# Third attention of a four-stage kernel: rounded scores of four row blocks interleaved, maxima in bf16, one subtraction instruction

## The chip, the cores and the metric

The kernel runs on one core of a Trainium2 chip. The metric is the time of one execution on the device in microseconds (us). One execution was also recorded by the hardware profiler; its rows are what this document reads. Engines are named as in the profile: PE is the matrix engine (PEld its weight loads), DVE the vector engine, ACT the scalar engine, POOL the GpSimd engine, SP the engine that issues most DMAs.

## The reference, cut to what matters

The model is a chain of small blocks: two convolution-like attentions, an attention with a top-2 mixture of experts, and then the layer that the change is in, an attention over 512 tokens with 8 heads of width 16, again followed by a mixture of experts. Here the batch is seen as 8 images of 256 tokens. The kernel does for each of the 8 images (b), each of the 8 heads (h):

```
scores  = (q / sqrt(16)) @ k.T            # 256 x 256, float32 in the matrix engine
scores  = round_to_bf16(scores)
p       = exp(scores - max(scores, row))  # bf16
p       = p / sum(p, row)                 # sum kept as bf16
out     = p @ v                           # then the output projection, added to t
```

On the chip's side one row of scores is 256 numbers that lie on one partition, and 128 rows are handled at once. A head of an image is two such row blocks; the kernel takes two heads together, so a unit of work is four row blocks of 128 x 256 numbers.

## The kernel before, in words

**Tiling.** The third attention is `block4`. Its unit is a step (b, g): image b of 8, group g of 4, where a group is two heads, that is four row blocks r = 0..3. There are 32 steps. `images()` writes the first image out, loops images 1 to 5 with a hardware loop of four steps, and writes the last two images out. Two buffers (index g % 2) hold scores `s3`, probabilities `p3` and transposed probabilities `pT3`.

**What each engine does in a step, in its program order:**

- PE: `scores` of three steps ahead (L1698, L1699), `values` of the step before (L1726), in some steps the output transposes and projection (L1735, L1741, L1745), `transposed` of this step (L1710), `project` of q or k for a later fragment (L1684 to L1686).
- ACT: `rounded` of two steps ahead, one ACTIVATE of 1024 numbers per partition that copies the scores out of the PSUM banks as bf16 into `s3` (L1616); in three steps of four `evacuate`, which copies the transposed probabilities out (L1632); `upper` (L1608); `exponentials` of the next step, four ACTIVATEs of 256 numbers, each with a row sum into `smb3` (L1625).
- DVE: `centre` of the next step (L1816 takes the maximum of the two halves of each row into `mxh3`, L1818 reduces that to four maxima in `mx3`, L1821 subtracts them from `s3`, one instruction for each row block); in one step of four `evacuate` (L1836); `normalise` of this step (reciprocal L1826, four multiplications L1829); `lower` (L1808 or L1810); and one of `gather` (L1844), `copy_out` (L1852), `add` (L1857).
- POOL: `split_values`, once for an image (L1585 to L1591).

**What orders them.** The engines run their own lists and wait on semaphores: `sb` (a rounded score group is there), `sub` (a subtraction is done), `ex` (an exponential is done), `p` (a normalised row block), `tp` and `pt` (transposed, copied out). `exponentials` waits for all four subtractions (`sub` at 4i + 4) before its first ACTIVATE; `transposed` waits for all four multiplications. In `centre` DVE waits for itself twice, for the halves' maxima and for the four maxima.

**Layout.** `s3` is `[P, 2, 2 * S, N]`, so for a buffer each partition holds row block 0's 256 bf16 numbers, then row block 1's, and so on. `mxh3` is `[P, 4, 128]` in bf16, `mx3` is `[P, 4, 4]` in float32.

Of the kernel before, what the change touches and what calls it, by code (L numbers as in the profile page):

```python
# [16 lines left out]
BF16 = mybir.dt.bfloat16  # L17
U32, I32 = mybir.dt.uint32, mybir.dt.int32
ALU = mybir.AluOpType
ACT = mybir.ActivationFunctionType  # L20
AX = mybir.AxisListType

P = 128
B = 8
N = 256
S = N // P
T = B * N
H, DH = 8, 16
# [68 lines left out]
def build(nc, a, out):  # L97
    ctx = ExitStack()
    with ctx:
# [3 lines left out]
        def sem(name):  # L103
            return ctx.enter_context(nc.semaphore(name))

        ps = ctx.enter_context(nc.psum_tensor("ps", [P, 8, CH], F32))

        def psb(bank):

            return ps[:, bank, :].bitcast(BF16)  # L110
# [47 lines left out]
        def own(name, shape, dt=F32):  # L158
            return room.enter_context(nc.sbuf_tensor(name, shape, dt))
# [37 lines left out]
        chv, chp = Chain(None, dve_s), Chain(None, pool_s)  # L197
# [40 lines left out]
        @block.sync  # L238
        def _(sp):
            early = AT["bias1"][1]  # L240
            sp.dma_start(w[:, 0:early], a["pack"][:, 0:early]).then_inc(s_w, 16)
            for p in range(L):
                sp.dma_start(xs[:, p, :].rearrange("c (b n) -> c b n", b=2),
                             a["x"][2 * p:2 * p + 2].rearrange("b c n -> c b n")).then_inc(m[f"xs{p}"], 16)
            sp.dma_start(w[:, early:], a["pack"][:, early:]).then_inc(s_w2, 16)
            sp.dma_start(braw, a["b12"]).then_inc(s_braw, 16)

            sp.wait_ge(s_still, 1)
            sp.dma_start(xs_d[0:1], still[0:1, 0:P]).then_inc(s_braw, 16)
            sp.wait_ge(s_braw, 32)  # L250
# [316 lines left out]
        def flat(banks):  # L567
            return banks.rearrange("p a b -> p (a b)")
# [351 lines left out]
        def pair_high(act, c, cs=c3):  # L920

            act.wait_ge(cs["tp"], c + 1)
            act.activation(xH[:, c * CH:(c + 1) * CH], pair_bank(c, cs), ACT.Copy).then_inc(cs["xh"], 1)
# [25 lines left out]
        def weighted_rows(act, layer, c):  # L949

            act.wait_ge(gathered[c], (layer + 1) * 16 * 2)
            for b in (2 * c, 2 * c + 1):
                for s in range(S):
                    x = act.activation(y_rows(1, s, b), y_rows(1, s, b), ACT.Copy, scale=gk[:, row(layer, s, b), 1:2])
            x.then_inc(y_weighted, 1)
# [20 lines left out]
        def place(layer, r):  # L976
# [5 lines left out]
                     act=NT, hm=0, ht=NT, hH=NT, hL=NT, yp=NT, yo=NT, fin=0, ftp=0, fo=0, fst=0, oh=0)  # L982
# [6 lines left out]
        def experts(layer, wHL, n_up, hid, gate_w, gate_b):  # L989
# [326 lines left out]
            def _(dve):  # L1316
# [196 lines left out]
        v3f = own("v3f", [P, B, S, P])  # L1513
        v3r = own("v3r", [P, 2, S, P])
        vp3 = own("vp3", [P, B, S, H, 3, DH], BF16)
        mx3 = own("mx3", [P, H // 2, 2 * S])
        sm3 = own("sm3", [P, H // 2, 2 * S])
        smb3 = own("smb3", [P, H // 2, 2 * S], BF16)
        mxh3 = own("mxh3", [P, 2 * S, P], BF16)
        s3 = own("s3", [P, 2, 2 * S, N], BF16)  # L1520
        p3 = own("p3", [P, 2, 2 * S, N], BF16)
        pT3 = own("pT3", [P, 2, 2, S, N], BF16)
        o3b = own("o3b", [P, S, P], BF16)
# [1 line left out]
        m3 = {n: sem("at3_" + n) for n in  # L1525
              "vp vf v0 vr v prj pru prl sp sb sub ex p tp pt op o otp ot fp done".split()}
# [3 lines left out]
        QKB, TB, SB, OB, FB = 0, 1, 2, 6, 7  # L1530

        def images(engine, step, around=None):


            for g in range(4):
                step(0, g, True)
            with engine.Fori(1, B - 2) as b:
                if around:
                    around(b)
                for g in range(4):  # L1540
                    step(b, g, False)
            if around:
                around(None)
            for b in (B - 2, B - 1):
                for g in range(4):
                    step(b, g, False)

        def there(b, g):

            return not isinstance(b, int) or b < B  # L1550
# [4 lines left out]
        def fragment(b, g, n):  # L1555

            return b + (g + n) // 4, (g + n) % 4 // 2, (g + n) % 2

        def ahead(b, g, n):

            return (b, g + n) if g + n < 4 else (b + 1, g + n - 4)
# [38 lines left out]
        @block4.scalar  # L1600
        def _(act):
            act.preload_act_table(ACT.Exp)

            def upper(b, g, part, bank=QKB):

                act.wait_ge(m3["prj"], 4 * b + 2 * g + part + 1)
                dst, scale = ((q3H, DH ** -0.5), (k3H, 1.0))[part]
                act.activation(dst[:, g, :], ps[:, bank, part * N:(part + 1) * N], ACT.Copy, scale=scale).then_inc(m3["pru"], 1)  # L1608

            def rounded(b, g):  # L1610

                i = 4 * b + g
                act.wait_ge(m3["sp"], i + 1)
                if not (isinstance(b, int) and i < 2):
                    act.wait_ge(m3["ex"], 4 * (i - 1))
                act.activation(s3[:, g % 2], ps[:, SB + 2 * (g % 2):SB + 2 * (g % 2) + 2, :].rearrange("p a (s n) -> p (a s) n", s=2), ACT.Copy).then_inc(m3["sb"], 1)  # L1616

            def exponentials(b, g):
                i = 4 * b + g
                act.wait_ge(m3["sub"], 4 * i + 4)  # L1620
                if not (isinstance(b, int) and i < 2):
                    act.wait_ge(m3["tp"], i - 1)
                with nc.allow_low_precision(reason="the reference's sum here is bfloat16; the accumulator itself is float32"):
                    for r in range(4):
                        act.activation(p3[:, g % 2, r, :], s3[:, g % 2, r, :], ACT.Exp, accum_out=smb3[:, g, r:r + 1]).then_inc(m3["ex"], 1)  # L1625

            def evacuate(b, g):
                i = 4 * b + g
                act.wait_ge(m3["tp"], i + 1)
                if not (isinstance(b, int) and i < 2):  # L1630
                    act.wait_ge(m3["op"], i - 1)
                act.activation(pT3[:, g % 2].rearrange("p h k n -> p (h k n)"), psb(TB), ACT.Copy).then_inc(m3["pt"], 1)  # L1632

            weighted_rows(act, 0, 0)
            weighted_rows(act, 0, 1)
            pair_high(act, 0)
            for n in range(4):
                upper(*fragment(0, 0, n), bank=n)
            weighted_rows(act, 0, 2)
            pair_high(act, 1)  # L1640
            weighted_rows(act, 0, 3)

            def values_out(c, n):

                act.wait_ge(m3["vp"], c + n)
                act.activation(v3f[:, 2 * c:2 * (c + n)].rearrange("p b s c -> p (b s c)"), flat(ps[:, 4 + c:4 + c + n, :]), ACT.Copy).then_inc(m3["vf"], 1)

            values_out(0, 2)
            rounded(0, 0)
            rounded(0, 1)  # L1650
            upper(*fragment(0, 0, 4))
            pair_high(act, 2)
            exponentials(0, 0)
            pair_high(act, 3)

            def step(b, g, first):
                if there(*ahead(b, g, 2)):
                    rounded(*ahead(b, g, 2))
                if g != 3 and not (first and g == 0):
                    evacuate(*((b, g - 1) if g else (b - 1, 3)))  # L1660
                if there(*fragment(b, g, 5)[:2]):
                    upper(*fragment(b, g, 5))
                if there(*ahead(b, g, 1)):
                    exponentials(*ahead(b, g, 1))
                if first and g == 0:
                    values_out(2, 1)
                    values_out(3, 1)
            images(act, step)
            evacuate(B - 1, 3)
# [130 lines left out]
        def _(dve):  # L1800
# [12 lines left out]
            def centre(b, g):  # L1813

                dve.wait_ge(m3["sb"], 4 * b + g + 1)
                chv.done(dve.tensor_tensor(mxh3[:], s3[:, g % 2, :, 0:P], s3[:, g % 2, :, P:N], ALU.max))  # L1816
                chv.wait()
                chv.done(dve.tensor_reduce(mx3[:, g, :], mxh3[:], AX.X, ALU.max))  # L1818
                chv.wait()
                for r in range(4):  # L1820
                    dve.tensor_scalar(s3[:, g % 2, r, :], s3[:, g % 2, r, :], mx3[:, g, r:r + 1], None, ALU.subtract).then_inc(m3["sub"], 1)  # L1821

            def normalise(b, g):

# [60 lines left out]
            summed(3)  # L1885
            pair_apply(dve, 2)
            centre(0, 0)
            lower(*fragment(0, 0, 4))
            pair_low(dve, 2)
# [106 lines left out]
```

## Time and profile before

| what | value |
|---|---|
| time, median of 3 runs | 628.43 us (628.04 to 632.07) |
| span of the profiled execution | 626.9 us |
| PE busy in it | 510.1 us (81%) |
| DVE busy | 433.2 us (69%) |
| ACT busy | 282.2 us (45%) |
| POOL busy | 285.7 us (46%) |
| third attention, first to last score matmul | 331.5 to 454.8 us |
| normalisations of the third attention | 342.1 to 466.5 us |

The span is what the profiler saw between the first and the last instruction; it stands 1.5 us under the median of the runs. Busy shares of the whole span mix stages that have different limits, so the page is followed into the stretch from 331 to 471 us, in which the changed code runs. A row of a timeline gives start and duration; "x4" means four instructions drawn as one, and what stands in brackets is how long the engine had been idle and what released it.

### The profile page before, as it was taken

Reading aid. Unit: us, or ns where it says so; the run is one execution under the profiler, and the core shown is the slowest. Engines: PE = TensorE matmul, PEld = TensorE weight load, DVE = VectorE, ACT = ScalarE, POOL = GpSimd, SP = SyncE. Lnnn points to the kernel's source line nnn. Section 1 sums busy time; section 2 is a strip of 40 time slices with the busy share of each in tenths; the row PEclk is TensorE's granted clock in tenths of the full one; section 3 lists DMA queues with packets and bytes.
Section 4 is the critical chain, followed back from the end, with each engine's and each line's share of the span. In section 5 each row is a group of like instructions: output and inputs, shape, how many; then the busy total and the mean of one; then the engine's idle time right before and its main releaser. Section 6 shows DMA issues by size and latency. Waiting matters only on the chain. (4 is left out here: it accounts for less than half of the span.)

```text
span 626.9 us, 10580 instructions
## 1 busy us (share of the span) xinstructions
PE 510.1 (81%) x3062; PEld 398.5 (64%) x3062; DVE 433.2 (69%) x1235; ACT 282.2 (45%) x754; POOL 285.7 (46%) x269
## 2 busy tenths in 40 slices
PE   9997995999657999999148899999857688777752
PEld 4685563868524999999147787777647346555531
DVE  2738559998885457444388799999997865555534
ACT  4523133300312764444235899999861023333314
POOL 1093438879244677774112111111111157777740
PEclk9798576989678999999665555555555779999985
DMA  6000070000541111121400000000004012221217
GB/s 224 1 1 2 0 269 0 1 2 0 209 127 31 47 52 49 53 52 36 134 18 1 2 2 0 0 0 0 1 2 122 12 34 51 56 51 51 51 41 199
DMA packets 26509, 31.08 MB, mean 50 GB/s; under 512 B 3105, under 2 KB 21538, under 8 KB 26338
## 3 DMA queue, kind: packets, MB, share of 16 engines
q1 hardware_dynamic: 21474, 20.29, 10.1%
q0 software_dynamic: 4992, 10.23, 6.4%
q8 instruction: 25, 0.41, 0.3%
q14 instruction: 18, 0.15, 0.1%
HBM read 20.16 MB, written 10.36 MB: 49 GB/s over the span
## 5 line engine op out<-in xcount | busy, mean ns | idle before, releaser
L1109 POOL DMA_INDIRECT rows_out<-yo,idy x78 | 77.8, 998 | 36.4 <-DVE yo L1477 19.6
L1103 POOL DMA_INDIRECT xg<-rows_in,idx x78 | 75.6, 969 | 36.7 <-issue 22.2
L1161 ACT ACTIVATE hraw<-ps 128x512 f32<-128x512 f32 (+1 forms) x78 | 38.3, 491 | 107.0 <-PE ps L1269 107.0
L1469 DVE TENSOR_TENSOR hidden<-ps,hidden 128x512 fp32r<-128x512 f32 (+1 forms) x78 | 43.3, 555 | 46.1 <-ACT hidden L1168 46.1
L1290 PE MATMUL ps<-wHL,hidden 128*128 x234 | 69.1, 347 | 6.1 <-issue 2.8
L1293 PE MATMUL ps<-wHL,hidden 128*128 x234 | 54.0, 231 | 0.0
L1290 PEld LDWEIGHTS ps<-wHL,hidden 128*128 128x128 f32 x234 | 44.0, 188 | 15.1 <-issue 14.8
L1625 ACT ACTIVATE p<-s 128x256 bf16<-128x256 bf16 x128 | 51.6, 413 | 3.3 <-DVE s L1821 3.3
L1585 POOL CAST vp<-v3f 128x256 bf16<-128x256 f32 x8 | 3.5, 441 | 95.8 <-ACT s L1616 95.8
L1267 PE MATMUL ps<-wHL,xa 128*128 x78 | 34.6, 444 | 13.9 <-issue 12.2
L1293 PEld LDWEIGHTS ps<-wHL,hidden 128*128 128x128 f32 x234 | 44.6, 190 | 0.0
L1464 DVE TENSOR_TENSOR hraw<-hraw,ps 128x256 f32<-128x256 f32 x39 | 16.4, 422 | 40.4 <-ACT hraw L1161 40.4
L1154 ACT ACTIVATE xa<-ps 128x128 fp32r<-128x128 f32 x78 | 22.0, 283 | 44.0 <-PE ps L1255 43.9
L1168 ACT ACTIVATE hidden<-ps 128x512 fp32r<-128x512 f32 (+1 forms) x78 | 37.8, 485 | 1.5 <-PE ps L1277 1.5
L1277 PE MATMUL ps<-w,hraw 128*128 128x128 f32 x234 | 38.3, 272 | 0.1
L1277 PEld LDWEIGHTS ps<-w,hraw 128*128 128x128 f32 x234 | 30.2, 140 | 10.5 <-DVE hraw L1464 0.2
L1477 DVE TENSOR_REDUCE yo<-ps 128x128 f32<-128x256 f32 x78 | 32.6, 417 | 6.2 <-PE ps L1293 5.9
L1710 PE MATMUL ps<-identb,p 128*128 128x128 bf16 x256 | 33.3, 311 | 4.2 <-DVE p L1829 3.6
L1616 ACT ACTIVATE s<-ps 128x1024 bf16<-128x1024 f32 x32 | 32.8, 1024 | 1.7 <-PE ps L1699 0.3
L1698 PE MATMUL ps<-k3S,q3H 32*128 32x256 f32 x128 | 32.4, 494 | 0.0
L565 PE MATMUL ps<-w 128*128 128x512 f32 x50 | 31.9, 798 | 0.3 <-PEq L525 0.3
L1829 DVE TENSOR_SCALAR p<-p,sm 128x256 bf16<-128x256 bf16 x128 | 30.7, 302 | 1.1
(287 smaller groups left out, 1388.6 us busy)
## 6 DMA issues: line engine op xcount, KB each, us to landing
wraw<-in_ex SPq DMA_DIRECT2D x2, 2048.0 KB, 9.9
rows_in<-both SPq DMA_DIRECT2D x8, 512.0 KB, 6.2
both<-rows_out SPq DMA_DIRECT2D x16, 256.0 KB, 4.2
wraw<-in_ex SPq DMA_DIRECT2D x1, 3072.0 KB, 12.7
w<-in_pack SPq DMA_DIRECT2D x1, 1582.0 KB, 8.4
xg<-rows_in,idx POOLq DMA_INDIRECT x78, 2.6
rows_out<-yo,idy POOLq DMA_INDIRECT x78, 2.3
xs<-in_x SPq DMA_DIRECT2D x4, 256.0 KB, 4.6
```

Source lines behind the costliest of these rows:

```text
L1103: pool.indirect_dma_start(xg[:, j % NXG, :], None, xs_d[:], bass.IndirectOffsetOnAxis(idx[:, j:j + 1], 0)).then_inc(ld[j % NXG], 16)
L1109: pool.indirect_dma_start(ys_d[:], bass.IndirectOffsetOnAxis(idy[:, j:j + 1], 0), yo[:, j % NYO, :], None).then_inc(st[j % NYO], 16)
L1161: act.activation(hraw[:, j % 2, :], ps[:, HB + j % 2, 0:hid], ACT.Gelu if layer == 0 else ACT.Silu).then_inc(z["act"], 1)
L1168: act.activation(hH[:, j % 2, :], ps[:, HTB + j % 2, 0:hid], ACT.Copy).then_inc(z["hH"], 1)
L1267: pe.matmul(o, xa[:, j % NX, :], wh, start=layer == 1, stop=False)
L1277: x = pe.transpose(ps[:, HTB + j % 2, h * P:(h + 1) * P], hraw[:, j % 2, h * P:(h + 1) * P], ident)
L1290: pe.matmul(o.rearrange("p (i n) -> p i n", i=2), hH[:, j % 2, h * P:(h + 1) * P], both, start=h == 0, stop=False)
L1293: x = pe.matmul(o[:, 0:P], hL[:, j % 2, h * P:(h + 1) * P], wHL[:, bass.ds(e, 1), 0, cols].rearrange("p a n -> p (a n)"), start=False, sto ...
L1469: dve.tensor_tensor(hL[:, j % 2, :], ps[:, HTB + j % 2, 0:hid], hH[:, j % 2, :].bitcast(F32), ALU.subtract).then_inc(z["hL"], 1)
L1616: act.activation(s3[:, g % 2], ps[:, SB + 2 * (g % 2):SB + 2 * (g % 2) + 2, :].rearrange("p a (s n) -> p (a s) n", s=2), ACT.Copy).then_in ...
L1625: act.activation(p3[:, g % 2, r, :], s3[:, g % 2, r, :], ACT.Exp, accum_out=smb3[:, g, r:r + 1]).then_inc(m3["ex"], 1)
L1710: x = pe.transpose(psb(TB)[:, ((h * S + kt) * S + s) * P:((h * S + kt) * S + s + 1) * P], p3[:, g % 2, h * S + s, kt * P:(kt + 1) * P], id ...
```

## The change

Three things change together, all in `block4`. The score tile is laid out with the four row blocks interleaved: number n of the four row blocks lies side by side, so that one row block's numbers are now 4 elements (8 bytes) apart. ACT's copy out of PSUM writes with that step, and each exponential reads with that step; the tile of half maxima `mxh3` is interleaved too, and the reduction reads it with the same step. The maxima `mx3` are stored in bf16 (a maximum of bf16 numbers is one of them). And the four subtractions, each with a per-partition scalar, become one tensor-tensor instruction over 1024 numbers, whose second operand is the row of four maxima, repeated 256 times by a step of 0. The semaphore `sub` is raised once in a step and not four times. `p3`, and all that comes behind it, keeps its layout.

```diff
-        mx3 = own("mx3", [P, H // 2, 2 * S])
+        mx3 = own("mx3", [P, H // 2, 2 * S], BF16)
-        mxh3 = own("mxh3", [P, 2 * S, P], BF16)
-        s3 = own("s3", [P, 2, 2 * S, N], BF16)
+        mxh3 = own("mxh3", [P, P, 2 * S], BF16)
+        s3 = own("s3", [P, 2, N, 2 * S], BF16)
...
 def rounded(b, g):
-    act.activation(s3[:, g % 2], ps[:, SB + 2 * (g % 2):SB + 2 * (g % 2) + 2, :].rearrange("p a (s n) -> p (a s) n", s=2), ACT.Copy).then_inc(m3["sb"], 1)
+    act.activation(s3[:, g % 2].rearrange("p n r -> p r n"), ps[:, SB + 2 * (g % 2):SB + 2 * (g % 2) + 2, :].rearrange("p a (s n) -> p (a s) n", s=2), ACT.Copy).then_inc(m3["sb"], 1)
...
 def exponentials(b, g):
-    act.wait_ge(m3["sub"], 4 * i + 4)
+    act.wait_ge(m3["sub"], i + 1)
...
     for r in range(4):
-        act.activation(p3[:, g % 2, r, :], s3[:, g % 2, r, :], ACT.Exp, accum_out=smb3[:, g, r:r + 1]).then_inc(m3["ex"], 1)
+        act.activation(p3[:, g % 2, r, :], s3[:, g % 2, :, r], ACT.Exp, accum_out=smb3[:, g, r:r + 1]).then_inc(m3["ex"], 1)
...
 def centre(b, g):
-    chv.done(dve.tensor_tensor(mxh3[:], s3[:, g % 2, :, 0:P], s3[:, g % 2, :, P:N], ALU.max))
+    chv.done(dve.tensor_tensor(mxh3[:], s3[:, g % 2, 0:P], s3[:, g % 2, P:N], ALU.max))
     chv.wait()
-    chv.done(dve.tensor_reduce(mx3[:, g, :], mxh3[:], AX.X, ALU.max))
+    chv.done(dve.tensor_reduce(mx3[:, g, :], mxh3[:].rearrange("p n r -> p r n"), AX.X, ALU.max))
     chv.wait()
-    for r in range(4):
-        dve.tensor_scalar(s3[:, g % 2, r, :], s3[:, g % 2, r, :], mx3[:, g, r:r + 1], None, ALU.subtract).then_inc(m3["sub"], 1)
+    dve.tensor_tensor(s3[:, g % 2], s3[:, g % 2], mx3[:, g, None, :].to_broadcast([P, N, 2 * S]), ALU.subtract).then_inc(m3["sub"], 1)
```

## Rows read from the trace of the kernel before

**Rows 1.** The page, part 2: busy tenths and TensorE clock in 40 slices of 15.7 us.
```profile
PE   9997995999657999999148899999857688777752
...
DVE  2738559998885457444388799999997865555534
ACT  4523133300312764444235899999861023333314
...
PEclk9798576989678999999665555555555779999985
```

**Rows 2.** Busy time by stretch: us, then PE, PEld, DVE, ACT, POOL, clock, DMA, GB/s.
```profile
340.00:355.00 15.00, 14.57 (x98) 12.99 (x97) 11.21 (x38) 11.77 (x34) 2.19 (x4) 0.50 0.00 1
...
460.00:475.00 15.00, 8.04 (x69) 5.57 (x68) 13.53 (x66) 5.15 (x16) 3.39 (x4) 0.50 0.01 2
...
370.90:432.30 61.40, 59.10 (x457) 48.30 (x455) 59.75 (x208) 57.16 (x167) 8.58 (x15) 0.50 0.00 0
```

**Rows 3.** Timeline of DVE: L1852 runs once an image; first and last of six.
```profile
365.86 0.28 DVE L1852 COPY oT<-ps 128x256 bf16<-128x256 bf16 x1
...
444.96 0.28 DVE L1852 COPY oT<-ps 128x256 bf16<-128x256 bf16 x1
```

**Rows 4.** Timeline, one step from 402.0 us, parts of DVE, ACT and PE.
```profile
402.00 0.41 DVE L1816 TENSOR_TENSOR mxh<-s 128x512 bf16<-128x512 bf16 x1
402.44 0.69 DVE L1818 TENSOR_REDUCE mx<-mxh 128x4 f32<-128x512 bf16 x1
403.16 0.88 DVE L1821 TENSOR_SCALAR s<-s,mx 128x256 bf16<-128x256 bf16 x4
...
403.95 0.68 DVE L1836 COPY pT<-ps 128x1024 bf16<-128x1024 bf16 x1
...
404.07 0.42 ACT L1625 ACTIVATE p<-s 128x256 bf16<-128x256 bf16 x1 [0.18 <-DVE s L1821]
...
405.68 0.77 PEld L1710 LDWEIGHTS ps<-identb,p 128*128 128x128 bf16 x8 [0.27 <-DVE p L1829]
```

**Rows 5.** Waits between 405 and 434 us: who waited for whom, us, times, longest.
```profile
PEld ps L1726 <- issue: 1.9, 7, 0.5
PEld ps L1710 <- DVE p L1829: 1.7, 6, 0.4
...
ACT p L1625 <- DVE s L1821: 0.5, 3, 0.2
```

**Rows 6.** Groups of instructions by line, DVE: count, busy us, mean ns, idle before.
```profile
L1821 DVE TENSOR_SCALAR s<-s,mx 128x256 bf16<-128x256 bf16 x128 | 28.9, 289 | 1.1
...
L1816 DVE TENSOR_TENSOR mxh<-s 128x512 bf16<-128x512 bf16 x32 | 13.7, 429 | 0.8 <-ACT s L1616 0.8
```

**Rows 7.** Single lines, DVE: duration in ns, min/median/max, first and last start.
```profile
L1816 DVE TENSOR_TENSOR mxh<-s x32: 407/416/639, 333.8 to 460.2; 128x512 bf16<-128x512 bf16 x32
L1836 DVE COPY pT<-ps x8: 682/683/692, 356.8 to 465.1; 128x1024 bf16<-128x1024 bf16 x8
L1396 DVE TENSOR_TENSOR lanes<-lane_of,iotab x8: 1209/1212/3291, 184.5 to 501.7; 128x1024 bf16<-128x1024 bf16 x8
L845 DVE TENSOR_TENSOR sc<-sc,mx x2: 691/692/693, 110.8 to 136.8; 128x512 f32<-128x512 f32 x2
```

**Rows 8.** Single lines, DVE reductions: L1353 and L1818 contiguous, L835 strided.
```profile
L1353 DVE TENSOR_REDUCE rk<-cmp x4: 685/686/686, 170.7 to 488.6; 128x64 f32<-128x512 f32 x4
L1818 DVE TENSOR_REDUCE mx<-mxh x32: 685/686/689, 334.5 to 460.7; 128x4 f32<-128x512 bf16 x32
L835 DVE TENSOR_REDUCE mx<-sc x2: 1076/1085/1094, 104.2 to 130.5; 128x64 f32<-128x512 f32 x2
```

**Rows 9.** Single lines, ACT: the rounding copy and the exponentials.
```profile
L1616 ACT ACTIVATE s<-ps x32: 1017/1024/1025, 332.8 to 457.3; 128x1024 bf16<-128x1024 f32 x32
L1625 ACT ACTIVATE p<-s x128: 398/416/438, 337.6 to 463.5; 128x256 bf16<-128x256 bf16 x128
```

## The prediction, made before the changed kernel ran

> **What bounds the kernel now.** I read the slices first. From about 330 to 485 us, where the third attention lies, PE, DVE and ACT all stand at 8 or 9 tenths, so the stage has no engine that is plainly alone at the limit, and the TensorE clock stands at 5 tenths, the lower of its two levels, 1.2 GHz [rows 1]. Then I took the loop apart. The output copy of an image starts at 365.86 us and, five images later, at 444.96 us, so an image takes 79.1 / 5 = 15.82 us and a step 3.955 us [rows 3]. The window 370.9 to 432.3 us is 61.4 / 3.955 = 15.5 steps. Of its 61.40 us DVE is busy 59.75, PE 59.10, ACT 57.16 [rows 2]. Per step that leaves idle: DVE 0.11 us, PE 0.15, ACT 0.27. DVE's rest is not waiting but the small gaps between instructions that wait for one another (0.03 us between L1816's end and L1818) [rows 4], and the list of waits has no row in which DVE waits there. PE and ACT do wait for DVE: weight loads for the normalised block 1.7 us, exponentials for the subtraction 0.5 us within 29 us (7.3 steps) [rows 5]; in the step shown they are the 0.27 and the 0.18 us in brackets [rows 4]. So DVE sets the pace, with PE and ACT close behind. In the stage's start (340 to 355 us) DVE is busy 11.2 of 15 us; in its tail (460 to 475 us) DVE 13.5 and PE only 8.0, so there DVE alone carries the end [rows 2].
>
> **The change, part by part.**
>
> The four subtractions. They are 128 instructions that cover 28.9 us, so 0.903 us for each of 32 steps [rows 6]; undisturbed a block is 0.88 us long and the next instruction starts 0.79 us after its start [rows 4]. All of it is removed from the pacing engine.
>
> The one subtraction. No tensor-tensor over 1024 bf16 numbers with this operand is in the trace, so it is bounded from both sides. Low bound: the pace of two numbers a cycle. L1816, a bf16 tensor-tensor over 512, takes 416 ns; a float32 one over 512 takes 692 (L845); the bf16 one over 1024 whose first operand repeats one number at an innermost step of 0 takes 1212 (L1396) [rows 7]. From 692 and 1212 one number costs (1212 - 692) / 512 = 1.02 ns and the fixed part is 172; at half that price 1024 numbers cost 172 + 520 = 692, and the 1024-number bf16 copy, which runs at that pace, does take 683 [rows 7]. High bound: 1212 ns, the slow pace. I take 0.69 us. L1396 has an operand that stands still at the innermost step; here the innermost step is 1 over four maxima and only the outer one is 0, so all three operands move like L1816's. The Trainium skill ("Vector Engine (DVE) Microarchitecture Reference", 5.1) says that with 2-byte operands a row read again and again still runs at two elements a cycle, and one element read again and again at one; L1396 agrees with its second half, and no run here shows the first. Saved per step: 0.903 - 0.69 = 0.21 us, over 32 steps 6.8 us of DVE. It also releases the exponentials 0.2 us earlier after the maxima.
>
> The halves' maximum (L1816) reads and writes runs of 512 contiguous numbers, as long as before: 0. The bf16 maxima are 4 numbers a step: 0.
>
> The strided reduction. L1818 reads 512 numbers at a step of 2 bytes in 686 ns; now the step is 8 bytes. The trace has one strided read of the tile kind: L835, steps of 32 bytes, 1085 ns for 512 numbers against 686 for L1353, the same shape contiguous [rows 8]. That is 399 / 512 = 0.78 ns for a number. Bounds: 0 to 0.40 us a step. L1818 shows in addition that bf16 numbers at 2 bytes go no faster than float32 ones at 4. I take 0.
>
> The strided write and reads of ACT. The rounding copy writes 1024 numbers (1.02 us), the four exponentials read 4 x 256 (416 ns each) [rows 9]. No row has ACT at a step over one element. With L835's 0.78 ns a number, each side would add up to 0.80 us a step. Bounds 0 to 1.60 us; I take 0. If it isn't 0, cover is 0.27 us of ACT's idle a step, and beyond it every tenth comes onto the path.
>
> What stands behind taking 0: 8 bytes lie nearer to L1353's 4 bytes, which are free, than to L835's 32. The Trainium skill bears on it with two rules. "SBUF — State Buffer" (Door 1) says that a line is 16 bytes and that two hits on a line are enough for the full rate; 8 bytes gives exactly two hits, 32 bytes none, and L835 agrees with the second half. "Vector Engine (DVE) Microarchitecture Reference" (5.2) says that a port keeps its full rate only on runs of two adjacent 4-byte words, which single bf16 numbers 8 bytes apart are not, and gives about 0.65 cycle for each other element; an estimate by it is 0.35 us more for the reduction. That rule speaks against this change; rivals 3 and 5 are its case, priced there from rows.
>
> **The sum.** In the loop DVE's step would fall from 3.955 to 3.74 us. ACT can't go under 3.955 - 0.27 = 3.68. PE's busy share leaves 3.955 - 0.15 = 3.80, but part of that busy time are matmuls drawn long while they wait, as its own waits for DVE's blocks are 1.7 / 7.3 = 0.23 us a step; so PE's floor is between 3.72 and 3.80. I take a saving of 0.17 a step (between 0.15 by PE and 0.21 by DVE) over the 24 steps of images 1 to 6: 4.1 us. Image 0: DVE idles a quarter of the time, I count half of four times 0.21: 0.4. Image 7, where DVE alone carries the end: three or four times 0.21: 0.8. Sum 5.3 us; nothing is added elsewhere, as the stage's successor starts from DVE's last work. Against the profiled span of 626.9 this is 621.6; the runs' median is 1.5 us above the span, so 623.1, and with some loss to new collisions of three engines that are all over 90% busy, **623.6 us** (0.8% faster).
>
> **The rivals.**
>
> 1. The steps are free, but PE's gaps don't close or the clock stays the limit: saving 0 to 0.1 us a step, 626 to 628. For it: PE is idle only 0.15 a step, and the weight loads' gaps named "issue" (1.9 us in 7.3 steps) don't hang on DVE [rows 5]. It is the same case as the forecast with a smaller size. Chance with the forecast: 0.60 together (0.42 for the forecast's size, 621.5 to 625.5; 0.18 for this).
> 2. PE's clock rises. At 1.2 GHz PE is 96% busy [rows 2]; were it granted 2.4, PE would leave the race, DVE's 0.21 would come through in full, and matmul latencies in the start and tail would shrink: 618 to 621. Against it: the stage holds 0.50 in every stretch, whatever PE's busy share (8.0 of 15 us or 14.6) [rows 2]. Chance 0.08.
> 3. Steps of 8 bytes cost on ACT (place: L1616's write or L1625's reads). With both at L835's price ACT's step is 3.68 + 1.60 = 5.28, 1.33 us over today's, for 30 steps: 40 us, 668. With one of them 3.68 + 0.80 = 4.48: 0.53 x 30 = 16 us, 644. With half that price on one, 4.08: 4 us slower, 632. It decides above 0.27 us a step, or 0.26 ns a number over 1024. For it: no row shows ACT with a step. Chance 0.21 (0.10 up to 640, 0.11 above).
> 4. The one subtraction runs at one number a cycle: 1.21 against 0.903, +0.31 us x 32 = 9.8, about 638. For it: L1396 does so, also with a step of 0, and a compiler may lay the operand out in another way. Chance 0.06.
> 5. Only the reduction pays for its step: 0.40 - 0.21 = +0.19 x 32 = 6 us, 634.5. Chance 0.05.
>
> **How the numbers follow.** The likeliest is 623.6. A measurement of this kernel can tell about 1%, 6.3 us, from no change. Faster by over 1% (under 622.1) needs nearly all of DVE's 6.8 us or the clock: 0.08 for rival 2 and 0.09 out of the forecast's size, 0.17. Slower by over 1% (above 634.7): rival 4, the greater part of rival 3 and half of rival 5: 0.06 + 0.17 + 0.03 = 0.26. Same: 0.57. The range must leave out 2 in 10: it leaves out the upper 0.11 of rival 3 and a part of rival 2 (0.05), and runs from 619.5 to 640. The forecast's own range is 621.5 to 628.
>
> **What would show it.** Right: L1821's four become one tensor-tensor of 680 to 700 ns; the reduction stays at 686, L1616 at 1024, L1625 at 416; the image period falls from 15.82 to 15.1 us; DVE's busy share falls from 97 to 94 or 95% and PE's waits for the normalised block shrink. Wrong: a subtraction near 1212 ns; a reduction above 750; an L1616 near 1800 or L1625 near 600 ns, with DVE waiting for the exponentials in the list of waits; a clock above 0.50 in the loop. If all durations are as forecast and the period stays at 15.8, PE's floor was the error.

## The result, and the profile after

The changed kernel takes 661.28 us (median of 4 runs, 660.78 to 664.11) against 628.89 us: the ratio is 1.0527, 95% interval 1.050 to 1.0554. It is 32 us slower, where 623.6 us was forecast and 640 was the upper end of the range. The span of its profiled execution is 659.3 us, against 626.9.

First what each changed instruction takes now, line by line, with duration in ns as min/median/max. They answer to [rows 7], [rows 8] and [rows 9]; below the changed code line numbers are smaller by one (L1820 is the one subtraction, L1828 the normalisation).

```profile
L1816 DVE TENSOR_TENSOR mxh<-s x32: 414/416/690, 334.9 to 493.0; 128x512 bf16<-128x512 bf16 x32
L1818 DVE TENSOR_REDUCE mx<-mxh x32: 685/686/687, 335.4 to 493.5; 128x4 bf16<-128x512 bf16 x32
L1820 DVE TENSOR_TENSOR s<-s,mx x32: 691/692/695, 336.1 to 494.2; 128x1024 bf16<-128x1024 bf16 x32
L1616 ACT ACTIVATE s<-ps x32: 2437/2457/2566, 332.4 to 488.7; 128x1024 bf16<-128x1024 f32 x32
L1625 ACT ACTIVATE p<-s x128: 411/437/469, 337.8 to 496.2; 128x256 bf16<-128x256 bf16 x128
```

Everything on DVE came out as forecast: the subtraction takes 692 ns (forecast 690), the reduction at a step of 8 bytes 686, as before. The exponentials, which read at 8 bytes, went from 416 to 437. The one large move is the rounding copy, which writes at a step of 8 bytes: 1024 ns before, 2457 now.

Then the pace. The output copy of an image (L1851 here) starts at these times; five images lie between the rows.

```profile
372.67 0.29 DVE L1851 COPY oT<-ps 128x256 bf16<-128x256 bf16 x1 [0.53 <-PE ps L1735]
...
473.05 0.29 DVE L1851 COPY oT<-ps 128x256 bf16<-128x256 bf16 x1
```

100.38 / 5 = 20.08 us an image, 5.02 a step, where before it was 15.82 and 3.955 [rows 3]. Busy time in just this stretch (us, then PE, PEld, DVE, ACT, POOL, clock):

```profile
372.67:473.05 100.38, 74.77 (x588) 62.09 (x587) 74.10 (x206) 99.63 (x214) 10.65 (x20) 0.50 0.00 0
```

ACT has no time left (99.63 of 100.38), and DVE, which held the pace before with 97% [rows 2], is busy 74%. A step of ACT grew from 3.68 to 99.63 / 20 = 4.98 us. The clock stays at 0.50. The list of waits between 405 and 434 us, to be held against [rows 5]:

```profile
PE ps L1726 <- ACT pT L1632: 8.7, 5, 1.9
DVE k3S L1810 <- ACT k3H L1608: 4.4, 3, 1.6
DVE q3L L1808 <- ACT q3H L1608: 2.6, 2, 1.3
```

All three end with ACT's work, and the waits for DVE's blocks are gone from the list. The copy of the transposed probabilities (L1632) stands on ACT's list behind the long rounding copy, and PE's `values` wait for it:

```profile
403.15 2.46 ACT L1616 ACTIVATE s<-ps 128x1024 bf16<-128x1024 f32 x1
...
405.32 1.14 ACT L1632 ACTIVATE pT<-ps 128x1024 bf16<-128x1024 bf16 x1
...
406.62 0.72 PE L1726 MATMUL ps<-vp,pT 128*128 x8 [1.90 <-ACT pT L1632]
```

### The profile page after: what moved, and what is told of

It reads as the page before. It is cut to its first block and busy times, and to the rows that moved or that the text cites. A ratio compares the mean times of both kernels' runs of the same rounds, so it can differ in the third digit from the quotient of the medians.

```text
span 659.3 us, 10469 instructions
## 1 busy us (share of the span) xinstructions
PE 511.0 (78%) x3062; PEld 400.4 (61%) x3062; DVE 428.0 (65%) x1139; ACT 325.1 (49%) x754; POOL 284.0 (43%) x269
## 5 line engine op out<-in xcount | busy, mean ns | idle before, releaser
L1616 ACT ACTIVATE s<-ps 128x1024 bf16<-128x1024 f32 x32 | 78.5, 2461 | 1.5 <-PE ps L1699 0.2
L1625 ACT ACTIVATE p<-s 128x256 bf16<-128x256 bf16 x128 | 53.8, 436 | 0.2 <-DVE s L1820 0.2
L1726 PE MATMUL ps<-vp,pT 128*128 (+1 forms) x256 | 18.7, 216 | 44.8 <-ACT pT L1632 40.5
L1290 PEld LDWEIGHTS ps<-wHL,hidden 128*128 128x128 f32 x234 | 44.1, 188 | 15.0 <-issue 14.8
L1726 PEld LDWEIGHTS ps<-vp,pT 128*128 128x128 bf16 x256 | 13.9, 113 | 54.3 <-issue 38.6
L1267 PE MATMUL ps<-wHL,xa 128*128 x78 | 34.6, 444 | 13.7 <-issue 13.4
L763 PE MATMUL ps<-w,pw 128*128 128x128 f32 x256 | 30.6, 284 | 3.4 <-DVE pw L596 3.4
```

Source lines behind the costliest of these rows:

```text
L1267: pe.matmul(o, xa[:, j % NX, :], wh, start=layer == 1, stop=False)
L1290: pe.matmul(o.rearrange("p (i n) -> p i n", i=2), hH[:, j % 2, h * P:(h + 1) * P], both, start=h == 0, stop=False)
L1616: act.activation(s3[:, g % 2].rearrange("p n r -> p r n"), ps[:, SB + 2 * (g % 2):SB + 2 * (g % 2) + 2, :].rearrange("p a (s n) -> p (a s) ...
L1625: act.activation(p3[:, g % 2, r, :], s3[:, g % 2, :, r], ACT.Exp, accum_out=smb3[:, g, r:r + 1]).then_inc(m3["ex"], 1)
```

## The experiments

The theory after the result (W): the write at a step of 8 bytes, and nothing else in the change, costs; the rest of the change is worth what was forecast. Twelve kernels were run. Their times (medians), each compared with runs of the kernel before on the same chip:

| run | edit | us | ratio to before | 95% interval |
|---|---|---|---|---|
| changed kernel | | 661.28 | 1.0527 | 1.050 to 1.0554 |
| e1_read_order | changed, copy walks the other way | 625.62 | 0.9958 | 0.9944 to 0.9971 |
| e2_steps | before, with single instructions at its end | 691.27 | | one run |
| e3_one_sub_old_layout | before, one subtraction | 638.54 | 1.016 | 1.0145 to 1.0176 |
| e4_pairs | interleaved in pairs | 628.94 | 1.0014 | 1.0003 to 1.0025 |
| e5_less_dve | e1, less DVE | 624.27 | 0.9928 | 0.9911 to 0.9945 |
| e6_less_pe | e1, less PE | 623.64 | 0.9924 | 0.9906 to 0.9941 |
| e7_after_more_dve | changed, more DVE | 663.42 | 1.0545 | 1.052 to 1.057 |
| e8_before_more_dve | before, more DVE | 643.09 | 1.0231 | 1.0214 to 1.0249 |
| e9_pool_later | e1, POOL later | 625.36 | 0.9955 | 0.9938 to 0.9972 |
| e10_upper_late | e1, ACT's order | 625.95 | 0.9959 | 0.9946 to 0.9972 |
| e11_upper_late_pool_later | e9 and e10 | 624.39 | 0.9937 | 0.9924 to 0.9951 |
| e12_less_act | e1, less ACT | 623.56 | 0.9934 | 0.9908 to 0.996 |

### e1_read_order: the same layout, written contiguously

```diff
-act.activation(s3[:, g % 2].rearrange("p n r -> p r n"), ps[...].rearrange("p a (s n) -> p (a s) n", s=2), ACT.Copy)
+act.activation(s3[:, g % 2], ps[...].rearrange("p a (s n) -> p n (a s)", s=2), ACT.Copy)
```

> The changed kernel, with one edit: the rounding copy walks number by number, so that it writes the interleaved tile contiguously and reads the PSUM banks at a step of 256 numbers (1 KB). Theory W (the write at a step of 8 bytes is what made the copy 2.46 us and the kernel slower; nothing else in the change costs): the copy is back near 1.02 us, an image's period falls from the changed kernel's value to 15.2 us or less (before: 15.82), time 622 to 626 us, ratio to before 0.990 to 0.996. Rival R (any interleaving walk costs ACT, the strided side only moves from write to read): the copy stays above 1.8 us, the time above 640 us. Rival P (PE is already at its floor at 1.2 GHz): the copy is 1.02 us but the time is within 0.3% of before.

```profile
L1616 ACT ACTIVATE s<-ps x32: 1018/1023/1026, 332.7 to 454.4; 128x1024 bf16<-128x1024 f32 x32
```

The copy is back at 1023 ns while it reads the PSUM banks at a step of 1 KB, and the time falls by 36 us, from 661.28 to 625.62. That undoes the whole loss and leaves the layout, the exponentials' strided reads, the strided reduction and the one subtraction in place. The first half of theory W holds, the write is what costs; rival R (any such walk costs ACT) falls. Against the kernel before it gains 0.42%, within the time that was expected, but its period is 15.39 us and not the 15.2 of the expectation, so the rest of the change is worth less than was forecast; e5, e6 and e9 to e12 are about that.

### e2_steps: each step alone

Single instructions behind the end of the kernel before, two of each. On its own engine each waits for the one ahead of it; ACT's list and DVE's run side by side, on different tiles. One of them, for a write step of 4 elements:

```python
act.activation(pdst[:, 0:4096].rearrange("p (r n k) -> p r n k", r=4, k=4)[:, :, :, 0],
               two.rearrange("p (r n) -> p r n", r=4), ACT.Copy)     # two: two PSUM banks, 1024 float32
```

> The kernel before, with a block of single instructions behind its end, each alone on its engine: ACT copies 1024 numbers from PSUM to bf16 at write steps of 2, 4, 8, 16 bytes, in the interleaved form and with the walk exchanged, and to float32 at 4, 8, 16 bytes; ACT reads bf16 at steps of 2 to 32 bytes; the same copies and reads on DVE and reductions of 512 numbers at read steps of 2 to 32 bytes. Theory W: ACT's writes jump from 1.0 to about 2.4 us at 8 bytes for bf16, and reads stay at 1.0 us up to 8 bytes and rise at 16 or 32. If what costs is a write narrower than its neighbour's 8-byte word, float32 at 8 bytes is slow as well; if what costs is a 2-byte write that can't be paired with the next, bf16 at 4 bytes is slow already (1.5 us or more) and float32 at 4 bytes is not. Rival: the copy alone takes 1.02 us at every step, and the 2.46 us come from DVE or PE touching the same memory. Time of the whole about 30 us plus a block's start above before.

ACT, 1024 numbers from PSUM, written as bf16 at steps of 2, 4, 8 and 16 bytes; then the changed kernel's interleaved form (L1959), the exchanged walk (L1962), and float32 written at 4, 8 and 16 bytes:

```profile
L1947 ACT ACTIVATE pdst<-ps x2: 1023/1023/1023, 639.6 to 664.4; 128x1024 bf16<-128x1024 f32 x2
L1950 ACT ACTIVATE pdst<-ps x2: 1303/1304/1304, 640.6 to 665.4; 128x1024 bf16<-128x1024 f32 x2
L1953 ACT ACTIVATE pdst<-ps x2: 2432/2432/2432, 642.0 to 666.8; 128x1024 bf16<-128x1024 f32 x2
L1956 ACT ACTIVATE pdst<-ps x2: 4692/4696/4699, 644.4 to 669.2; 128x1024 bf16<-128x1024 f32 x2
L1959 ACT ACTIVATE pdst<-ps x2: 2448/2448/2449, 649.2 to 674.0; 128x1024 bf16<-128x1024 f32 x2
L1962 ACT ACTIVATE pdst<-ps x2: 1023/1024/1024, 651.7 to 676.5; 128x1024 bf16<-128x1024 f32 x2
L1965 ACT ACTIVATE pdst<-ps x2: 1023/1024/1024, 652.7 to 677.5; 128x1024 f32<-128x1024 f32 x2
L1968 ACT ACTIVATE pdst<-ps x2: 1073/1077/1081, 653.8 to 678.6; 128x1024 f32<-128x1024 f32 x2
L1971 ACT ACTIVATE pdst<-ps x2: 1980/1980/1980, 654.9 to 679.7; 128x1024 f32<-128x1024 f32 x2
```

ACT reading bf16 from SBUF at steps of 2, 8 and 16 bytes:

```profile
L1974 ACT ACTIVATE pdst<-psrc x2: 1057/1057/1057, 656.9 to 681.7; 128x1024 bf16<-128x1024 bf16 x2
...
L1980 ACT ACTIVATE pdst<-psrc x2: 1123/1124/1126, 659.1 to 683.9; 128x1024 bf16<-128x1024 bf16 x2
L1983 ACT ACTIVATE pdst<-psrc x2: 2052/2053/2054, 660.2 to 685.0; 128x1024 bf16<-128x1024 bf16 x2
```

DVE: writes from PSUM to bf16 at 2 bytes (L1996), 8 (L2002) and 16 (L2005); copies from bf16 in SBUF written at 2 (L2008), 8 (L2014) and 16 bytes (L2017), and read at 8 (L2041); reductions of 512 numbers read at 8 (L2026) and 16 bytes (L2029):

```profile
L1996 DVE CAST pdst<-ps x2: 1225/1225/1225, 639.6 to 662.9; 128x1024 bf16<-128x1024 f32 x2
...
L2002 DVE CAST pdst<-ps x2: 2420/2420/2420, 642.2 to 665.5; 128x1024 bf16<-128x1024 f32 x2
L2005 DVE CAST pdst<-ps x2: 4679/4680/4681, 644.6 to 668.0; 128x1024 bf16<-128x1024 f32 x2
L2008 DVE COPY pdst<-psrc x2: 427/428/429, 649.3 to 672.7; 128x1024 bf16<-128x1024 bf16 x2
...
L2014 DVE COPY pdst<-psrc x2: 1301/1302/1302, 650.6 to 673.9; 128x1024 bf16<-128x1024 bf16 x2
L2017 DVE COPY pdst<-psrc x2: 2435/2444/2452, 651.9 to 675.3; 128x1024 bf16<-128x1024 bf16 x2
...
L2026 DVE TENSOR_REDUCE pdst<-psrc x2: 686/686/686, 655.8 to 679.2; 128x4 bf16<-128x512 bf16 x2
L2029 DVE TENSOR_REDUCE pdst<-psrc x2: 1048/1054/1059, 656.6 to 679.9; 128x4 bf16<-128x512 bf16 x2
...
L2041 DVE COPY pdst<-psrc x2: 694/695/696, 660.0 to 683.3; 128x1024 bf16<-128x1024 bf16 x2
```

The interleaved write takes 2448 or 2449 ns with PE idle and DVE at work on another tile, the first time beside DVE's copies from the contiguous one on (L2008, from 649.3), the second beside its widest writes (L2014 and L2017, from 673.9). The exchanged walk takes 1024 beside L2017 too (651.7 and 651.9). So the cost goes with the instruction and not with its neighbour, and the collision rival falls, as it does by e1, where the neighbours are at work as before. Writes and reads differ. A bf16 write from PSUM costs 1.0, 1.3, 2.4 and 4.7 us at 2, 4, 8 and 16 bytes: from 4 bytes on it grows nearly with the bytes that the write covers. Float32 at 8 bytes is nearly free, at 16 it is 1.98 us. Of the two readings that the expectation offered for 8 bytes, the write that is narrower than its neighbour's 8-byte word is out, since float32 at 8 bytes isn't slow, and bf16 at 4 bytes is already slow (1304), less so than the 1500 ns named there. DVE takes nearly ACT's times from PSUM (2420 and 4680 ns), so the cost isn't ACT's alone. But it isn't a price of the write alone either: from bf16 in SBUF the same writes take DVE 1302 and 2444 ns, about half. Why is not shown, and ACT has no such run. Reads at 8 bytes are free in the reduction (686) and cost ACT 6% (1124 against 1057); at 16 bytes the reduction takes 1054 ns and ACT 2053. They are not free for DVE's fast copy, which takes 695 ns at 8 bytes against 428. The whole took 63 us over before and not the 30 expected.

### e3_one_sub_old_layout: the subtraction alone

```diff
-for r in range(4):
-    dve.tensor_scalar(s3[:, g % 2, r, :], s3[:, g % 2, r, :], mx3[:, g, r:r + 1], None, ALU.subtract).then_inc(m3["sub"], 1)
+dve.tensor_tensor(s3[:, g % 2], s3[:, g % 2], mx3[:, g, :, None].to_broadcast([P, 2 * S, N]), ALU.subtract).then_inc(m3["sub"], 1)
```

Only the instruction is shown; the maxima are stored in bf16 here too, and `sub` is raised once in a step.

> The kernel before with its own layout, and only the four subtractions made one tensor-tensor, whose maxima are repeated at an innermost step of 0. Theory: the instruction runs at one number a cycle, 1.21 us in place of 0.90, so DVE, which sets the pace, needs 0.3 us more a step: period 16.9 us an image, time 636 to 639 us, ratio 1.012 to 1.018. Rival (PE or ACT sets the pace, DVE has hidden slack): under 631 us.

```profile
L1820 DVE TENSOR_TENSOR s<-s,mx x32: 1224/1225/1333, 335.4 to 471.7; 128x1024 bf16<-128x1024 bf16 x32
```

1225 ns with the maximum repeated at an innermost step of 0, against 692 with the four maxima as innermost row. So the interleaved layout is what makes the one instruction worthwhile: without it the same edit costs 10 us (638.54). The time is as expected; the period, 17.37 us ((454.02 - 367.19) / 5), is 0.5 above what was expected.

### e4_pairs: a step of 4 bytes

```diff
-s3 = own("s3", [P, 2, N, 2 * S], BF16)
+s3 = own("s3", [P, 2, 2, N, 2], BF16)          # pair, number, row block of the pair
```

> The changed kernel with row blocks interleaved in pairs and not in fours: the copy writes and the exponentials read at a step of 4 bytes, the subtraction's maxima are rows of two. Theory W with a cost that sets in at 8 bytes: the copy stays near 1.02 us, the subtraction at 0.69, time 622 to 626 us. With a cost for every bf16 write that isn't contiguous: the copy is 1.5 to 2.4 us, and ACT's step of 3.68 us grows by the same; at 1.5 us the time is 633 us, at 2.4 us 660 us.

```profile
L1616 ACT ACTIVATE s<-ps x32: 1306/1317/1327, 332.4 to 457.6; 128x1024 bf16<-128x1024 f32 x32
L1820 DVE TENSOR_TENSOR s<-s,mx x32: 691/692/799, 334.9 to 462.0; 128x1024 bf16<-128x1024 bf16 x32
```

Busy time of its five images, in the order of columns used above:

```profile
366.18:445.23 79.05, 74.95 (x588) 62.07 (x587) 74.52 (x206) 76.62 (x214) 11.32 (x20) 0.50 0.00 0
```

The copy is at 1317 ns, between the two cases that were written down. DVE saves as much as in e1 (74.52 us busy for five images, 74.49 in e1), but ACT is now busy 97% and an image takes 15.8 us as before: ACT's 0.29 us a step eat DVE's gain, and the time is before's to within 0.25% (628.94). That is about the size at which ACT's cover is used up.

### e7_after_more_dve and e8_before_more_dve: who sets the pace

```diff
 chv.done(dve.tensor_tensor(mxh3[:], ..., ALU.max))
 chv.wait()
+chv.done(dve.tensor_tensor(mxh3[:], ..., ALU.max))
+chv.wait()
```

> The changed kernel with the maximum of the halves taken twice (the same result): 0.44 us more of DVE in each of 32 steps, 14 us in all. If ACT alone sets the changed kernel's pace (it is busy 102.5 of 103.5 us in the loop, DVE 76): the time stays at 660 to 663 us. Rival (DVE's chain through the maxima is on the path too): 665 to 675 us.

> The kernel before with the maximum of the halves taken twice (the same result): 0.38 to 0.42 us more of DVE a step. If DVE sets the pace of the kernel before: nearly all of 32 x 0.40 = 13 us comes through, 640 to 642 us. If DVE only ties with the others and has slack: under 636 us.

The same extra 0.42 us of DVE a step costs 14.8 us in the kernel before (643.09 against 628.25), a little more than was expected, and 2 us in the changed one (663.42, whose interval overlaps the changed kernel's). The 663.42 lie between the two cases written down for e7; in the loop hardly anything moved, as its first five output copies are 20.18 us apart, against 20.14 in the changed kernel. So DVE set the pace before, as the prediction said, and in the changed kernel ACT does.

### e5, e6, e12, e9, e10, e11: what stops the corrected kernel

Each starts from e1. e5 leaves out the halves' maximum on DVE (the reduction sees the first half of each row only), e6 the low product of the scores on PE, e12 the row sums on ACT, for which a constant stands; e9 delays POOL, e10 moves ACT's `upper`, e11 does both:

```diff
 # e9, e11
-pool.wait_ge(m3["sb"], 4 * b + 1)
+pool.wait_ge(m3["p"], 16 * (b - 1) + 12)
 # e10, e11: in the fourth step of an image
-upper, exp 0, exp 1, exp 2, exp 3
+exp 0, exp 1, upper, exp 2, exp 3
```

> The kernel with the read order exchanged (the rounding copy writes contiguously), and without the maximum of the two halves (L1816): the reduction takes the first half of each row only, so the second half is left out of the maxima. That takes 0.42 us of DVE out of each step, 1.66 us of an image. There an image took 15.36 us. If DVE still sets the pace alone: the period falls to about 13.9 us (time 612 to 615 us). If PE at 1.2 GHz is at its floor: the period stays at 15.2 to 15.4 us (time 624 to 626 us). ACT's own work is 14.66 us an image, so with DVE out of the way it can't go under that.

> The kernel with the read order exchanged, and with the second of the two score products (q's low part, L1699) left out, 4 of 8 score matmuls a step, about 0.8 us of PE a step. If DVE sets the pace: period 15.2 to 15.4 us, time within 1.5 us of the kernel with the read order exchanged. If PE does: the period falls to where DVE or ACT stop it, 14.7 to 15.0 us, time 621 to 623 us.

> The kernel with the read order exchanged, and the exponentials leave out the row sums (the sums stand at a constant, so the probabilities aren't normalised rightly): ACT loses the four accumulator reads, about 0.1 us each on its list, 0.35 us a step, 1.4 us an image. Theory A: the period falls from 15.36 to what DVE holds, 14.7 to 15.0 us, time 622 to 624 us. Rival: 625 to 626 us. With this run all three engines have been relieved one at a time.

Busy time of e1, e5, e6 and e12 between 366 and 441 or 442 us, each from its own trace:

```profile
366.00:441.00 75.00, 73.78 (x569) 60.72 (x568) 72.72 (x199) 71.49 (x208) 11.72 (x20) 0.50 0.00 0
```
```profile
366.00:442.00 76.00, 73.53 (x586) 61.30 (x585) 67.34 (x185) 72.50 (x214) 11.32 (x20) 0.50 0.00 0
```
```profile
366.00:442.00 76.00, 67.23 (x504) 53.24 (x503) 73.58 (x205) 72.35 (x215) 11.66 (x20) 0.50 0.00 0
```
```profile
366.00:441.00 75.00, 72.14 (x583) 58.68 (x582) 72.95 (x205) 67.12 (x136) 13.09 (x20) 0.52 0.00 0
```

In e1 PE is busy 98%, DVE 97%, ACT 95%. From four image periods each (starts of the first to the fifth output copy) the period is 15.39 us in e1, 15.34 in e5, 15.42 in e6, 15.18 in e12. Relieving DVE by 1.66 us an image brings 0.05, relieving PE (its busy share falls from 98 to 88%) brings nothing, relieving ACT brings 0.2. No single engine holds it: with DVE relieved (89% busy) ACT's list is full but for one wait of 0.55 us an image on PE's projection; with PE (88%) or ACT (89%) relieved DVE is at 97% again, as in the kernel before. The clock in e12 isn't what helped: it rose (to 0.84) between 415 and 420 us only, and that image's period is 15.16 like its neighbours'. So the branches of the expectations that named one engine as the limit all fell short: e5 met the period that was written down for PE's floor, but e6 shows that it isn't PE alone, and e12 stopped at 15.18 where 14.7 to 15.0 was expected. What fits all four is a tie of two lists: DVE's with its small gaps, and right behind it ACT's, whose 3.68 us of work a step and 0.14 of that wait are 3.82 of 3.85. The times fall by more than the periods (e6 is 2.0 us under e1, e5 1.4), since the part before the loop is shorter too: the first output copy starts at 364.08 us in e6, 364.97 in e5 and 365.72 in e1.

> The kernel with the read order exchanged, and POOL starts its split of an image's values when DVE has finished the normalisation of a step (semaphore p) instead of when ACT has rounded the scores of the next image (sb): about 1.3 us later, so that it lies beside DVE's reductions and not beside L1828. Theory C (a quarter of DVE's gain is given back because L1828 is stretched while POOL runs, 0.88 to 1.49 us once an image): all L1828 are near 281 ns, the period falls by 0.25 to 0.5 us from 15.36, time 623 to 624.5 us. Rival (PE's floor): L1828 is short again and the period stays.

The normalisation of five images in the kernel before (365.86 to 444.96 us, with the four subtractions), then in e1, then in e9 with the one subtraction (count, busy us, mean ns):

```profile
L1829 DVE TENSOR_SCALAR p<-p,sm 128x256 bf16<-128x256 bf16 x80 | 19.2, 302 | 0.7
L1821 DVE TENSOR_SCALAR s<-s,mx 128x256 bf16<-128x256 bf16 x80 | 18.2, 291 | 0.7
```

```profile
L1828 DVE TENSOR_SCALAR p<-p,sm 128x256 bf16<-128x256 bf16 x80 | 20.6, 320 | 0.7
```
```profile
L1828 DVE TENSOR_SCALAR p<-p,sm 128x256 bf16<-128x256 bf16 x80 | 17.5, 282 | 0.7
...
L1820 DVE TENSOR_TENSOR s<-s,mx 128x1024 bf16<-128x1024 bf16 x20 | 14.4, 719 | 0.7
```

The normalisation is indeed stretched beside POOL's work, and more in e1 (20.6 us) than before (19.2 us in the same five images). Moving POOL takes 3.1 us out of it and puts 0.6 into the subtraction and 0.9 into the maxima (L1816: 458 ns, 415 in e1). The time (625.36) and the period (15.35) are nearly those of e1, so theory C fails: DVE is relieved, and ACT's busy share and its wait of 0.55 us an image are as they were. e10 took that wait away and got another in its place:

> The kernel with the read order exchanged, and in the fourth step of an image ACT rounds q (upper, L1608) between the second and third exponential instead of ahead of the first, so that it doesn't wait 0.55 us there for PE's projection. Theory A (after the exchange ACT's own list, 14.65 us of work and that wait, holds an image at 15.2 to 15.4 us, whatever DVE or PE are relieved of): the wait is gone and the period falls by 0.2 to 0.5 us, time 623 to 624.5 us (DVE's 14.9 us stops it). Rival (three engines collide, no one list holds): no change, 625 to 626 us.

```profile
404.10 0.44 ACT L1627 ACTIVATE p<-s 128x256 bf16<-128x256 bf16 x1 [0.73 <-DVE s L1823]
```

The row is of e10, where the exponentials are L1627 and the subtraction L1823. ACT now arrives before the subtraction is done; period 15.55, time 625.95: no gain, as the rival had it. Then both together:

> Both: ACT's q rounding between the exponentials, and POOL's split after DVE's normalisation. Theory A: 0.2 to 1 us below the kernel with the first alone, as DVE, next in line, isn't stretched in L1828 any more: 622.5 to 624 us. Rival: as before, 625 us.

624.39 us, ratio 0.9937 (0.9924 to 0.9951), period 15.32, just above the 622.5 to 624 of theory A. It is the fastest kernel here that computes everything, 0.6% ahead of the kernel before and 5.6% ahead of the changed one; its lead over e1 (0.9958, 0.9944 to 0.9971) is within the intervals' overlap, so that part is not shown.

## Why the prediction was wrong, point by point

**What bounds the kernel: right.** DVE set the pace with PE and ACT close behind. e8 shows it: DVE's added time came through whole, 14.8 us for 32 x 0.42 = 13.4.

**The one subtraction: right.** 692 ns against 690 forecast; e3 gives the other end, 1225 ns, which was rival 4's case. The Trainium skill's rule ("Vector Engine (DVE) Microarchitecture Reference", 5.1), that a row read again and again keeps two elements a cycle and one repeated element doesn't, is now shown by rows here: 692 and 1225 ns.

**The strided reduction: right.** 686 ns, unchanged.

**The strided reads of ACT: nearly right.** 416 to 437 ns, at most 0.08 us a step and not 0. ACT's busy time doesn't show it: 73.57 us in five images before, 73.30 in e1.

**The strided write of ACT: this step failed.** The prediction said: "Bounds 0 to 1.60 us; I take 0", with each side, write and reads, at most 0.80 us a step from L835's 0.78 ns a number. The write alone cost 1.43 us a step (2457 against 1024), 1.40 ns a number. Two things in the step were wrong. The value: 0 was chosen by comparing 8 bytes with L1353's 4 and L835's 32, both reads. And the bound for one side: L835 is a read of float32 and says nothing of a bf16 write, which costs more at 8 bytes (2432 ns for 1024) than float32 writes at 16 (1980). That the bound for both sides together, 1.60, holds the measured 1.43 + 0.08 is luck: the write took nearly all of it. No row that the prediction shows has an engine write single 2-byte numbers apart, so the write had no bound from a row of its kind. Of the two rules of the Trainium skill that were weighed, the one of 16-byte lines ("SBUF — State Buffer", Door 1) agrees with the reduction's and ACT's reads (free or nearly so at 8 bytes, 1054 and 2053 ns at 16) and with the float32 writes (1077 at 8, 1980 at 16), but not with the bf16 write, slow at 4 and 8 bytes already. The rule of two adjacent words ("Vector Engine (DVE) Microarchitecture Reference", 5.2) predicted a loss at 8-byte reads that the reduction doesn't have. Neither gives the size of the 2-byte write.

**Rival 3 was the case, at another size.** Its place was right (L1616 on ACT) and so was its rule, that beyond 0.27 us a step every tenth comes onto the path: e4, with 0.29 us more, is level with before. Its price for one side, 0.80 us and 644 us, was too small; its 0.11 above 640 us held the result. ACT's step grew by 1.30 us (3.68 to 4.98), less than 1.43 and 0.08 together: the next instruction starts 0.29 us before the long copy's end (2.17 us after its start, in the rows above), where before it did so by 0.10. Less the 0.27 us of cover that is 1.03; the period rose by 1.07 a step. Over 30 steps this is 32 us, the measured loss.

**The sum for the gain: nearly twice too large.** With the write repaired (e1) the gain was 2.8 us of the median, not 5.3. Busy time of five images (columns as above) in the kernel before and in e1:

```profile
365.86:444.96 79.10, 75.96 (x587) 62.02 (x586) 77.00 (x266) 73.57 (x217) 11.93 (x20) 0.50 0.00 0
```
```profile
365.72:442.53 76.81, 75.54 (x588) 62.00 (x587) 74.49 (x206) 73.30 (x216) 11.72 (x20) 0.50 0.00 0
```

DVE is busy 97% in both, and the five images are 2.29 us shorter while DVE's work fell by 2.51. So what was mis-sized first is DVE's own saving, 0.13 us a step and not 0.21. The subtractions did fall by 0.22 (18.2 to 13.8 us in 20 steps), but 0.07 of it went back into the normalisation, stretched beside POOL (20.6 against 19.2 us); the small rest has no one row. ACT's floor is the second: its idle 0.27 us a step was counted as free, but 0.14 of it (0.55 us an image) is a wait for PE's projection that stays when everything else is shorter. That e5 and e9, with DVE relieved further, gain next to nothing in the loop agrees with this.

## What to carry to other kernels

Before interleaving a bf16 tile for the sake of its reader, look at who writes it: walk the writer so that it writes contiguously and let the stride fall on a read, on PSUM above all, where a step of 1 KB was free here. A price taken from a read row doesn't bound a write; if no row has the operation's kind, put the width into the range or measure one instruction alone first. When three engines are busy 93 to 97%, look for what takes a saving back: here about half of it came through, and relieving one engine further only handed the pace to the next.

## What the runs showed of the hardware

- bf16 writes to SBUF from PSUM at steps of 2, 4, 8 and 16 bytes take 1.02, 1.30, 2.43 and 4.70 us for 1024 numbers on ACT, and 2.42 and 4.68 at the last two on DVE. Float32 at 4, 8 and 16 bytes: 1.02, 1.08, 1.98. From bf16 in SBUF, DVE's writes at 2, 8 and 16 bytes take 0.43, 1.30 and 2.44.
- bf16 reads from SBUF are at or near full rate up to a step of 8 bytes in a reduction (686 ns for 512) and on ACT (1.06 to 1.12 us for 1024), and slower at 16 (1054 ns and 2.05 us). DVE's copy takes 0.70 us for 1024 at 8 bytes against 0.43 contiguous. PSUM read by ACT at a step of 1 KB is free (1024 ns).
- Beside POOL's work DVE's single-source bf16 instructions and its two-source ones are stretched (up to 780 ns for 281 in e8, and 886 for 692 in e12), but the reduction of the maxima (L1818 in the kernel before) never took over 689 ns.
